# Four moved unpack steps and one dropped wait in a two-layer feed-forward kernel

## The reference

```python
x = x + L0_ffn(L0_cond(x, ids0))      # layer 0
x = x + L1_ffn(L1_cond(x, ids1))      # layer 1

def _L0_ffn_ref(x, qweight_gu, ..., qweight_down, ...):
    w_gu = _dequant(qweight_gu, qzeros_gu, scales_gu, g_idx_gu)   # 512 x 2752, 4 bits each
    inter = jnp.einsum('bsh,hf->bsf', x, w_gu)
    gate, up = (inter[..., :INTER], inter[..., INTER:])           # INTER = 1376
    h = jax.nn.silu(gate) * up
    w_d = _dequant(qweight_down, qzeros_down, scales_down, g_idx_down)   # 1376 x 512
    return jnp.einsum('bsf,fh->bsh', h, w_d)

def _dequant(qw, qz, sc, g_idx):      # W[i,j] = sc[g[i],j] * (wq[i,j] - (zq[g[i],j] + 1))
    ...
```

## Time and profile before

| | |
|---|---|
| median of 3 runs | 443.33 us (443.18 to 443.56) |
| the profiled execution's own time | 443.33 us |
| span of its trace | 441.5 us, 1.83 us less than its own time |
| PE busy | 436.8 us (99%) |
| DVE busy | 334.7 us (76%) |
| ACT busy | 223.1 us (51%) |
| POOL busy | 213.2 us (48%) |
| chain of work that ended last | PE 95%, DVE 2%, issue 1%, ACT 1% |

### The profile page before, as it was taken

The page is one execution under the profiler, slowest core; times in us unless marked ns, Lnnn a source line. Parts: engine busy times, 40 slices in busy tenths (PEclk is TensorE's granted clock), DMA queues, the critical chain, the costliest instruction groups (busy, mean ns, idle before and its releaser), DMA issues.

```text
span 441.5 us, 5486 instructions
## 1 busy us (share of the span) xinstructions
PE 436.8 (99%) x1942; PEld 357.0 (81%) x1942; DVE 334.7 (76%) x406; ACT 223.1 (51%) x293; POOL 213.2 (48%) x181
## 2 busy tenths in 40 slices
PE   8999999999999999999999999999999999999997
PEld 4688888888877888888888888888888888888886
DVE  5678999798887855746778568878688678999922
ACT  5416465665555433344677656466466554474200
POOL 0466788889988602400015778897987300000000
PEclk9999999999999999999999999999999999999999
DMA  8954024211223656585279517938469136986623
GB/s 287 248 186 150 25 71 138 85 36 19 25 24 95 168 205 272 207 317 191 96 261 341 208 69 240 307 133 277 163 214 287 56 132 261 351 289 181 224 101 143
DMA packets 29449, 78.20 MB, mean 177 GB/s; under 512 B 2480, under 2 KB 15936, under 8 KB 27760
## 3 DMA queue, kind: packets, MB, share of 16 engines
q1 hardware_dynamic: 25392, 66.08, 43.3%
q0 software_dynamic: 3456, 11.09, 9.4%
q10 hardware_dynamic: 576, 0.72, 0.5%
HBM read 57.15 MB, written 20.73 MB: 176 GB/s over the span
## 4 chain that ended last, share of the span: by engine, by line
PE 95%; DVE 2%; issue 1%; ACT 1%; ACTq 0%; DVEq 0%
PE ps L1946 10%; PE ps L1947 10%; PE ps L1948 10%; PE ps L1691 8%; PE ps L1692 8%; PE ps L1695 8%; PE ps L1814 5%; PE ps L1815 5%; PE ps L1816 5%; PE ps L2059 5%; PE ps L2061 5%; PE ps L2060 5%; PE ps L1929 2%; PE ps L1927 2%; PE ps L1928 2%
## 5 line engine op out<-in xcount | busy, mean ns | idle before, releaser
L1128 DVE TENSOR_TENSOR ring_lo<-raw,ring_hi 128x1792 fp32r<-128x1792 f32 (+3 forms) x24 | 50.0, 2088 | 13.4 <-ACT ring_hi L764 13.3
L1946 PE MATMUL ps<-zt_hi,ring_hi 128*128 128x512 f32 x140 | 54.6, 390 | 0.0
L1948 PE MATMUL ps<-zt_hi,ring_lo 128*128 128x512 f32 x140 | 54.6, 390 | 0.0
L1947 PE MATMUL ps<-zt_lo,ring_hi 128*128 128x512 f32 x140 | 54.6, 390 | 0.0
L764 ACT ACTIVATE ring_hi<-raw 128x1792 fp32r<-128x1792 f32 (+1 forms) x23 | 37.9, 1648 | 19.8 <-PE ps L1948 10.1
L637 POOL DMA_INDIRECT scale<-in_sc_gu,idx_gu x20 | 24.5, 1224 | 22.9 <-DVE idx_dn L1165 15.3
L673 POOL TENSOR_TENSOR raw<-raw 128x256 f32<-128x256 f32 x21 | 27.4, 1305 | 15.4 <-DMA raw<-in_gu 10.4
L1692 PE MATMUL ps<-h_lo,d_hi 128*128 128x512 f32 x88 | 34.3, 390 | 0.0
L1691 PE MATMUL ps<-h_hi,d_hi 128*128 128x512 f32 x88 | 34.3, 390 | 0.0
L1946 PEld LDWEIGHTS ps<-zt_hi,ring_hi 128*128 128x128 f32 x140 | 26.3, 188 | 5.9 <-issue 0.2
L1948 PEld LDWEIGHTS ps<-zt_hi,ring_lo 128*128 128x128 f32 x140 | 26.3, 188 | 5.5
(11 more groups left out here) (257 smaller groups left out, 1187.6 us busy)
## 6 DMA issues: line engine op xcount, KB each, us to landing
ad_raw<-in_w1T SPq DMA_DIRECT2D x8, 1024.0 KB, 4.9
wd<-down_weights SPq DMA_DIRECT2D x7, 1024.0 KB, 5.7
down_weights<-dhi SPq DMA_DIRECT2D x7, 896.0 KB, 4.6
down_weights<-dlo SPq DMA_DIRECT2D x7, 896.0 KB, 4.1
raw<-in_gu SPq DMA_DIRECT2D x12, 512.0 KB, 3.6
wd<-down_weights SPq DMA_DIRECT2D x7, 768.0 KB, 6.4
draw<-in_d SPq DMA_DIRECT2D x7, 512.0 KB, 4.4
res<-in_xT SPq DMA_DIRECT2D x1, 2048.0 KB, 7.9
```

Of the source, the lines that this page charges most:

```text
L1128: dve.tensor_tensor(dst, src, hi_part.bitcast(F32), ALU.subtract).then_inc(done_sem, 1)
L1946: pe.matmul(ps[:, bank, :], ring1_hi[s][:, w], z_hi[:, t], start=first and k == 0, stop=False, skip_group_check=True)
L1947: pe.matmul(ps[:, bank, :], ring1_hi[s][:, w], z_lo[:, t], start=False, stop=False, skip_group_check=True)
L1948: ins = pe.matmul(ps[:, bank, :], ring1_lo[s][:, w], z_hi[:, t], start=False, stop=k == 1, skip_group_check=True)
```

## The change

It does two things. SyncE no longer waits for TensorE to be done with the plain tiles before it starts the load of `nib_dn`. And three of the five steps `dequant_dn` stand elsewhere in VectorE's order: steps 0 and 1 stood behind `y_mul_1(9)` and stand now in front of `h_split(8)` and in front of `y_c_22(9)`; step 2 stood behind the whole loop and stands now in front of `y_c_22(10)`. No instruction is added or removed.

```diff
             sp.wait_ge(s_zk, 16)
             sp.wait_ge(s_zdk, 16)
-            sp.wait_ge(s_ring, len(PLAIN))
             sp.dma_start(nib_dn[:, :], a["qw_dn"]).then_inc(s_qd, 16)
...
                 if i == 9:
                     add_zeros_dn()
                 y_c_11(i)
+                if i == 9:
+                    dequant_dn(0)
                 h_split(i - 1)
                 y_c_12(i)
+                if i == 9:
+                    dequant_dn(1)
+                if i == FT0 - 1:
+                    dequant_dn(2)
                 y_c_22(i)
                 y_mul_1(i)
-                if i == 9:
-                    dequant_dn(0)
-                    dequant_dn(1)
-            dequant_dn(2)
             dequant_dn(3)
```

## The result

| | before | changed |
|---|---|---|
| median | 443.31 us (443.18 to 443.56, 6 runs) | 447.5 us (445.92 to 449.84, 6 runs) |
| ratio | | 1.0106, 95% interval 1.0081 to 1.0132 |
| profiled execution | 443.33 us, span 441.5 | 447.72 us, span 445.9 |
| TensorE's mean granted clock, profiled | 1.000 | 0.996 |

The change makes the kernel slower by 1.06%: 4.7 us, by the interval 3.6 to 5.9. Forecast were 446.0 us, 0.6% slower, in a range up to 447.7; 443.33 times the ratio is 448.0, just beyond it. The sign was right, the pause of TensorE came where it was forecast and with nearly its forecast length, and what is missing is the price of rival (b), the clock.

A forecast was written before the change was run, and what follows sets the result against it. TensorE, busy 436.8 of 441.5 us, was taken as the bound. The 441.5 us span plus 2.65 for steps 0 and 1, other terms at nothing, plus 1.83 around it gave 446.0 us, range 445.3 to 447.7.

The forecast's parts named there:

- rival (b): Tile 9: TensorE's clock falls in the pause, costing 2.7 us more (middle of 1.8 and 3.6), 448.7 us; chance 0.09.
- What bounds the kernel: Whole kernel: TensorE, busy 436.8 of 441.5 us, has no later slack, so any wait is paid in full.
- Steps 0 and 1: Tile 9: two unpack steps and a gather wait ahead of y_c_22(9) make TensorE start 2.65 us later.
- Rival (a): Tile 9: step 1's gather lands late, making TensorE 4.15 us later, 447.5 us in all; chance 0.09.
- Step 2: Tile 10, ahead of y_c_22(10): costs nothing, some 0.8 us of slack left; up to 0.5 with a late gather.
- the load: Near the start: the earlier nib_dn load fits mostly into free transfer time; costs nothing, at most 2.1 us.
- what comes back: Tile 9: y_mul_0(9) follows y_p_4(9) at once, which saves TensorE nothing.
- (c): Near the start: the early load delays the zg gathers and TensorE, 1.0 us on top, 447.0 us; chance 0.06.
- (d): Faster: less competition with scale gathers at 66 to 70, both y_c_22 waits go, 1.16 us gained, 442.2; chance 0.03.
- (e): Tile 9: no difference, y_c_22(9) is later but TensorE is not, its wait being for something else; chance 0.04.

The follow-up runs named there:

- e3: Kernel before with only unpack step 0 moved in front of h_split(8): 444.74 us, ratio 1.0034.
- e7: Kernel before with five idle additions on VectorE in front of y_c_22(9), nothing unpacked earlier: 447.23 us, ratio 1.0084.
- e9: Kernel before with three idle additions on VectorE in front of y_c_22(9): 444.79 us, ratio 1.0019.
- e6: Kernel before with nibbles_dn (tile 7) and add_zeros_dn (tile 9) moved in front of the same tile's w_lo: 441.90 us, ratio 0.9965.
- e4: Changed kernel with twelve matmuls, result unread, added in TensorE's queue before y_p_4(9)'s wait for y_c_22(9): 446.28 us, ratio 1.0071.
- e12: Changed kernel with six matmuls, result unread, added in TensorE's queue before y_p_4(9)'s wait for y_c_22(9): 448.23 us, ratio 1.0094.
- e5: Kernel before with only unpack step 2 moved in front of y_c_22(10): 443.56 us, ratio 1.0001.
- e2: Kernel before with only SyncE's wait for the plain tiles removed, so nib_dn loads early: 443.61 us, ratio 1.0007.
- e8: Kernel before with eight idle additions on VectorE in front of y_c_22(9): 449.44 us, ratio 1.0137.
- e1: Changed kernel with SyncE's wait for the plain tiles put back, so only the unpack steps move: 447.87 us, ratio 1.0109.
- e11: Kernel before with nibbles_dn and add_zeros_dn moved in front of w_lo, plus the early load of nib_dn: 442.61 us, ratio 0.9979.
- e10: Changed kernel with add_zeros_dn moved in front of w_lo in tile 9: 449.92 us, ratio 1.0131.

## Why the prediction was right or wrong

**What bounds the kernel: right.** TensorE has no slack, and each delay of `y_c_22(9)` shows in the time: e3 for one step, e7 to e9 for plain delays, and in the other direction e6, where both waits of the earlier trace rows go.

**Steps 0 and 1: right, a little small.** Forecast was TensorE at 146.01, measured 146.18; 2.65 us more pause against 2.81. The 0.16 that is missing is the landing of the gather (4.3 us after its start for 4.1, step 1 at 144.21 for 144.05). The executions of the changed kernel with a steady clock took 446.3 in the middle, for 446.0. Rival (a) is the same term with a later gather; e4 and e12 show one (an idle of 0.85 and 0.99 for 0.46), and it moved TensorE's restart by tenths, not by the 1.5 us that (a) priced.

**Step 2, the load, what comes back: right.** e5 and e2 show no difference, and in the changed kernel's trace TensorE has no new wait but one of 0.2 us near the start, at 5.24, which e3 and e8 have as well, without the early load. The load went out at 24.84 (forecast 23.9), and VectorE took the zero points at 34.02, against 34.12 in the earlier trace rows.

**The clock: the step that failed.** The sum put the clock's term at nothing; it stood in the text as rival (b) with a chance of 0.09 and a price of 2.7 us, and outside the range. It came true in 12 of the 16 recorded executions. Its price was 1.85 us (446.3 to 448.15) in eight of them and 3.0 (to 449.3) in four, so of the two figures named there 1.8 was about right and 3.6 somewhat high, and the chance was wrong. Of the 2.0 us between 446.0 and 448.0 the gather's landing makes 0.16 and the clock nearly all of the rest: 1.61 in the trace, 1.6 from e1 to e4, 1.3 in e7. Rival (b) had taken its price from the pace of the matmuls at the start. The granted clock reads 1.00 there in every window of the first 12 us, in the trace of before as in the changed kernel's, so for the start the profile shows the slow pace but not a lower clock beside it; behind the pause both are there. Two arguments were put against it. "The pauses of 0.5 us left the clock where it was" is no evidence about one of 3.1. "The pause is short" had no row behind it: apart from the 1.2 us at the very start the trace of before has no idle time of TensorE's on VectorE above 0.5 us, and so couldn't speak for the chance that I gave. With a chance of a half or more the forecast would have been near 448, which is 443.33 times the measured ratio.

**The rivals.** (c), (d) and (e) didn't come true: e2 and the trace against (c), the wait of 3.7 us against (d) and (e). The mechanism looked for in (d), both waits of `y_p_4` gone, is real, but what brought it about was work taken from between `w_lo` and `y_c_22` (e6, without the load).

## What to carry to other kernels

Work that is moved "into the shadow" of a bound engine was free here where, at that place, the engine's queue held other work ahead of the instruction that reads the result: step 2 was free behind twelve matmuls, and steps 0 and 1 were paid in full. Where a change makes TensorE stand still for microseconds, price the pause and the clock behind it, as two terms, and if no pause of that length is in the trace give the clock an even chance. To find a place that is free, look for where the helping engine itself waits: two other instructions, `nibbles_dn` and `add_zeros_dn`, moved into VectorE's idle time gained 0.35% (e6).

## What the runs showed of the hardware

What TensorE did before its clock fell: how long it stood still in each profile (from the time at which its next matmul was due), and in how many executions the mean clock was 0.996 or less. All the others have 0.999 or 1.000.

| kernel | stood still, us | clock fell |
|---|---|---|
| e6 | no wait for `y_c_22` | 0 of 7 |
| e11 | no wait for `y_c_22` | 1 of 10 |
| before, e2, e5 | 0.7 | 0 of 77 |
| e4, twelve matmuls in the pause | 0.9 | 0 of 4 |
| e3 | 1.6 | 0 of 5 |
| e9 | 1.9 | 0 of 10 |
| e12, six matmuls in the pause | 2.4 | 7 of 10 |
| e7 | 2.8 | 4 of 4 |
| e1 | 3.1 | 4 of 4 |
| changed | 3.3 | 12 of 16 |
| e10 | 3.4 | 4 of 4 |
| e8 | 4.2 | 4 of 4 |

The lengths are those of the one profiled execution. In e7 to e9 VectorE waits for no transfer in front of `y_c_22(9)`, so there they should hold for all executions, and these are the cleanest rows: 1.9 us never, 2.8 and 4.2 always. In the changed kernel, e1, e4, e10 and e12 the landing of a gather moves the length from one execution to the next, so it isn't known how long TensorE stood still in the 4 of 16 that kept their clock. I had not expected a fall after 2.4 or 2.8 us. The one of e11 has no pause in its profile to go with it and stays unexplained.

In each of the six profiles with a fall, the clock falls only after work has begun again: 0.3 to 0.5 us after in e1, e7, e10 and e12, 1.3 us in e8 and 1.4 us in the changed kernel (146.18 to about 147.55, by windows of half a microsecond). It then stays down for about 3.4 us in all six (mean granted clock 0.83 from 144 to 154), which costs half of that, 1.7. A mean clock of 0.992 stands for about twice the time (0.008 x 446 / 0.5 = 7.1), but no such execution was profiled, and its price isn't settled: 3.0 us by the middles of the changed kernel, in e1 no more than 0.3 above the others. What decides between these is left open. The Trainium skill (TensorE: Matmul & The Clock Gate, Part 1) says that activity releases the slow clock; e4 agrees, where useless matmuls keep the clock up and save 1.6 us against e1.
